# Layer 0's opening cut by batch: batch 0's keys and queries first, the rest among the attention units

## The reference

```python
x = x + _L0_xattn_ref(_layernorm(x), ctx_4096, ctx_4096, Wq, bq, Wk, bk, Wv, bv, Wo, bo)

Q = query @ Wq + bq; K = key @ Wk + bk; V = value @ Wv + bv   # 32 heads of 16; 8 key heads
scores = einsum('bhgqd,bhkd->bhgqk', Q, K) * scale
w = softmax(scores, axis=-1)
y = einsum('bhgqk,bhkd->bqhgd', w, V).reshape(B, S, EMBED)
return y @ Wo + bo
```

## Time and profile before

| | us |
|---|---|
| median of 3 runs | 1238.02 |
| fastest, slowest run | 1235.65, 1238.74 |
| the profiled execution's own time | 1236.24 |
| its span, first to last instruction | 1234.6 |
| TensorE busy | 1184.4 (96%) |
| VectorE, ScalarE, GpSimd busy | 818.9, 671.0, 404.5 |

### The profile page before, as it was taken

The page is one execution under the profiler, slowest core; times in us unless marked ns, Lnnn a source line. Parts: engine busy times, 40 slices in busy tenths (PEclk is TensorE's granted clock), DMA queues, the critical chain, the costliest instruction groups (busy, mean ns, idle before and its releaser), DMA issues.

```text
span 1234.6 us, 16581 instructions
## 1 busy us (share of the span) xinstructions
PE 1184.4 (96%) x5948; PEld 914.7 (74%) x5948; DVE 818.9 (66%) x1543; ACT 671.0 (54%) x1562; POOL 404.5 (33%) x483
## 2 busy tenths in 40 slices
PE   8989889899999999899999999999999999999997
...
PEclk9899999999999999899999999999999999999999
...
GB/s 290 173 172 134 139 91 103 284 217 102 153 203 253 150 147 181 86 59 60 60 44 69 43 61 69 61 52 54 69 59 50 44 69 60 61 69 27 59 1 68
DMA packets 72849, 127.93 MB, mean 104 GB/s; under 512 B 11640, under 2 KB 30968, under 8 KB 70072
## 3 DMA queue, kind: packets, MB, share of 16 engines
...
...
## 4 chain that ended last, share of the span: by engine, by line
PE 80%; DVE 8%; DMA 5%; ACT 3%; issue 3%; SPq 1%; ACTq 0%; POOL 0%; POOLq 0%; DVEq 0%
PE bank L466 49%; PE bank L1198 11%; PE bank L1986 7%; PE bank L1962 4%; PE bank L678 2%; PE bank L1258 2%; PE bank L692 1%; DMA q0st<-m0T 1%; PE bank L2301 1%; PE bank L1219 1%; PE bank L644 1%; DMA wf_raw<-in_wffn,weight_row 1%; PE bank L659 1%; DMA x<-in_x 1%; DVE den L895 1%
## 5 line engine op out<-in xcount | busy, mean ns | idle before, releaser
L1954 POOL TENSOR_SCALAR p<-p,mx 128x256 f32<-128x256 f32 x256 | 163.2, 654 | 522.0 <-DVE mx L1948 522.0
L1165 DVE TENSOR_TENSOR wf_lo<-wf_raw,wf_hi 128x512 fp32r<-128x512 f32 x188 | 121.7, 690 | 33.4 <-ACT wf_hi L1159 28.6
L1940 ACT ACTIVATE p<-bank,mx 128x256 f32<-128x256 f32 x256 | 118.0, 485 | 10.7 <-DVE mx L1930 10.6
L466 PE MATMUL bank<-xnA_hi,w1q_hi 128*128 128x512 f32 x288 | 118.8, 413 | 3.7 <-DVE xnA_lo L460 3.2
L1159 ACT ACTIVATE wf_hi<-wf_raw 128x512 fp32r<-128x512 f32 x192 | 110.2, 626 | 9.0 <-DMA wf_raw<-in_wffn,weight_row 9.0
L466 PE MATMUL bank<-xnA_hi,w1q_lo 128*128 128x512 f32 x288 | 115.0, 399 | 0.0
L466 PE MATMUL bank<-xnA_lo,w1q_hi 128*128 128x512 f32 x288 | 114.4, 397 | 0.0
L1969 ACT ACTIVATE p1T_hi<-bank 128x512 fp32r<-128x512 f32 x128 | 75.1, 596 | 65.7 <-PE bank L1962 65.7
L1894 ACT ACTIVATE q1T_hi<-bank 128x512 fp32r<-128x512 f32 x64 | 38.2, 597 | 132.5 <-PE bank L466 132.5
L1900 DVE TENSOR_TENSOR q1T_lo<-bank,q1T_hi 128x512 fp32r<-128x512 f32 x64 | 44.2, 691 | 93.2 <-ACT q1T_hi L1894 93.2
L466 PE MATMUL bank<-w1o_hi,a1T_hi 128*128 128x512 f32 x256 | 105.2, 411 | 0.1
...
## 6 DMA issues: line engine op xcount, KB each, us to landing
w_raw<-in_wq SPq DMA_DIRECT2D x64, 256.0 KB
w_raw<-in_wo SPq DMA_DIRECT2D x64, 256.0 KB
moe<-xn SPq DMA_DIRECT2D x2, 2304.0 KB, 11.7
...
q0st<-q_rows SPq DMA_DIRECT2D x14, 256.0 KB, 4.7
x<-in_x SPq DMA_DIRECT2D x8, 256.0 KB, 5.2
...
q_rows<-q0T_hi ACTq DMA_DIRECT2D x8, 256.0 KB
```

The costliest lines, as they stand in the source:

```text
L466: ins = nc.tensor.matmul(ps, a, b, start=(n == 0), stop=(n == len(pairs) - 1))
L1165: nc.vector.tensor_tensor(wf[m % 2][1][:, a, c, :], raw[m % STREAMS][:, a, c, :], wf[m % 2][0][:, a, c, :].bitcast(F32), ALU.subtract).the ...
L1940: ins = nc.scalar.activation(pr1[s % 2][:, h, :], banks.of(("s1", s, n))[:, hh * 2 * P:(hh + 1) * 2 * P], ACT.Exp, bias=m[:, UH + h:UH + h ...
L1954: ins = nc.gpsimd.tensor_scalar(pr1[s % 2][:, h, :], pr1[s % 2][:, h, :], m[:, 3 * UH + h:3 * UH + h + 1], 1.0, ALU.mult, ALU.mult)
```

## The change

Layer 0's opening is cut into three pieces in place of two halves (`PIECES`): batch 0 alone, batches 1 to 3, batches 4 to 7. Tile 0 is normalised and turned alone, and its keys and four query blocks (128 columns wide) are multiplied, stored and loaded back before tiles 1 to 3 are normalised. Then follow batches 1 to 3 (blocks of 384 columns), of which the fourth query block stands behind unit 2. All four values of the first half and the turning of the second half's tiles stand behind the first batch's maxima, the second half's keys behind unit 9, its queries behind units 11, 15, 19 and 22, its values behind units 23 to 26. The statistics of the second half's tiles stand between the maxima of units 3 to 6 on VectorE, the rounding of the output weights between the first exponentials on ScalarE. SP's loads are ordered by this, and those of x and of the context for the second half are issued behind batch 0's keys and queries.

```diff
--- before.py
+++ after.py
-        QUERY_AT = {KV0 + 2: 1, KV0 + 4: 2, LEAD_S + 5: 3}
-        QUERY_OUT_AT = {3: 0, KV0 + 3: 1, KV0 + 5: 2, LEAD_S + 6: 3}
+        QUERY_AT = {KV0 + 3: 0, KV0 + 7: 1, KV0 + 11: 2, KV0 + 14: 3}
+        OUT_WEIGHT_AT = {KV0 + 4 + k: k for k in range(KT)}
+        KEYS_AT, STATS1_AT = KV0 + 1, 3
...
+        PIECES = [(0, 0, P), (0, P, HT), (1, 0, HT)]
+        KEY_STORED, QUERY_STORED = ("st_q3", "st_k", "st_k"), ("st_q2", None, "st_q_half1")
...
-            for b in range(HB):
-                load(x[:, b, :], A["x"][b]).then_inc(S[f"rows_in{b}"], 16)
-            load(wq[:, :, :], A["wq0"]).then_inc(S["ld_wq0"], 16)
+            load(x[:, 0, :], A["x"][0]).then_inc(S["rows_in0"], 16)
             load(wkv[:, 0], A["wkv0"][:, 0]).then_inc(S["ld_wk0"], 16)
-            load(ctxT[0][:, :, :], A["ctxT"][0]).then_inc(S["ld_ctx00"], 16)
+            load(ctxT[0][:, :, 0:P], A["ctxT"][0, :, :, 0:P]).then_inc(S["ld_wk0"], 16)
             load(bq[:, :], A["bq0"]).then_inc(S["ld_bqk0"], 16)
             load(bk[:, :], A["bk0"]).then_inc(S["ld_bqk0"], 16)
+            load(wq[:, :, :], A["wq0"]).then_inc(S["ld_wq0"], 16)
+            for b in range(1, HB):
+                load(x[:, b, :], A["x"][b]).then_inc(S[f"rows_in{b}"], 16)
+            load(ctxT[0][:, :, P:HT], A["ctxT"][0, :, :, P:HT]).then_inc(S["ld_ctx00"], 16)
             load(wkv[:, 1], A["wkv0"][:, 1]).then_inc(S["ld_wv0"], 16)
...
-            for b in range(HB, B):
-                load(x[:, b, :], A["x"][b]).then_inc(S["ld_x_rest"], 16)
-            load(ctxT[1][:, :, :], A["ctxT"][1]).then_inc(S["ld_ctx01"], 16)
-            load(bo[:, :], A["bo0"].broadcast_to([P, D])).then_inc(S["ld_wbo0"], 16)
-            load(wo_raw[:, :, :], A["wo0"]).then_inc(S["ld_wbo0"], 16)
...
+            keys_in(0)
+            queries_in(0)
+            for b in range(HB, B):
+                load(x[:, b, :], A["x"][b]).then_inc(S["ld_x_rest"], 16)
+            load(ctxT[1][:, :, :], A["ctxT"][1]).then_inc(S["ld_ctx01"], 16)
             keys_in(1)
             queries_in(1)
             maxima(0)
+            load(bo[:, :], A["bo0"].broadcast_to([P, D])).then_inc(S["ld_wbo0"], 16)
+            load(wo_raw[:, :, :], A["wo0"]).then_inc(S["ld_wbo0"], 16)
...
-        VALUES_AT = {KV0 - 1: (HB, HB + 1), KV0: (HB + 2,), KV0 + 1: (HB + 3,)}
+        VALUES_AT = {3 * KV0 - 1 + k: HB + k for k in range(HB)}
...
-            for k in range(HB):
+            norm_turn(0, 0, 0)
+            keys(0, 7)
+            for m, n in enumerate((4, 5, 6, 0)):
+                query(0, m, n)
+            for k in range(1, HB):
                 norm_turn(0, k, k)
-            query(0, 0, 4)
-            query(0, 1, 5)
-            keys(0, 7)
-            query(0, 2, 0)
-            query(0, 3, 1)
-            for b, n in enumerate((2, 3, 4, 5)):
-                values(b, n)
-            for k, n in enumerate((7, 2, 3, 4)):
-                norm_turn(1, k, n)
             keys(1, 5)
-            query(1, 0, 7)
+            for m, n in enumerate((7, 2, 3)):
+                query(1, m, n)
             for i in range(-LEAD_S, UNITS0 - KV0 + ADD_LAG + 1):
                 if i + LEAD_S < UNITS0:
                     scores(i + LEAD_S)
                 if 0 <= i + LEAD_T < UNITS0:
                     turned_scores(i + LEAD_T)
                 j = i + LEAD_S
-                for b in VALUES_AT.get(j, ()):
-                    values(b, b - HB + 2)
+                if j == 2:
+                    query(1, KT - 1, 4)
                 if j == KV0 - 1:
                     maxima(0)
+                    for b, n in enumerate((2, 3, 4, 5)):
+                        values(b, n)
+                    for k, n in enumerate((7, 2, 3, 4)):
+                        norm_turn(1, k, n)
+                if j == KEYS_AT:
+                    keys(2, 5)
                 if j in QUERY_AT:
-                    query(1, QUERY_AT[j], 7)
+                    query(2, QUERY_AT[j], 7)
+                if j in VALUES_AT:
+                    values(VALUES_AT[j], next(srs))
...
-            norm_sqrt(0)
-            for k in range(HB):
-                norm_hi(0, k)
-            query(0, 0)
-            act.wait_ge(S["q0_lo"], 1)
-            queries_out(nc.scalar, 0, 0)
-            query(0, 1)
-            act.wait_ge(S["q0_lo"], 2)
-            queries_out(nc.scalar, 0, 1)
+            norm_sqrt(0, 0, 1)
+            norm_hi(0, 0)
             keys(0)
             act.wait_ge(S["k0_lo"], 1)
             keys_out(nc.scalar, 0)
-            norm_sqrt(1)
-            query(0, 2)
-            act.wait_ge(S["q0_lo"], 3)
-            queries_out(nc.scalar, 0, 2)
-            for k in range(KT // 2):
-                out_weight(k)
-            query(0, 3)
-            act.wait_ge(S["q0_lo"], 4)
-            queries_out(nc.scalar, 0, 3)
-            for k in range(KT // 2, KT):
-                out_weight(k)
-            for k in range(HB):
-                norm_hi(1, k)
+            for m in range(KT):
+                query(0, m)
+                act.wait_ge(S["q0_lo"], m + 1)
+                queries_out(nc.scalar, 0, m)
+            norm_sqrt(0, 1, HB)
+            for k in range(1, HB):
+                norm_hi(0, k)
             keys(1)
-            query(1, 0)
+            act.wait_ge(S["k0_lo"], 2)
+            keys_out(nc.scalar, 1)
+            for m in range(KT - 1):
+                query(1, m)
+                act.wait_ge(S["q0_lo"], KT + m + 1)
+                queries_out(nc.scalar, 1, m)
             for i in range(-LEAD_S, UNITS0 - KV0 + ADD_LAG + 1):
                 if 0 <= i + LEAD_T < UNITS0:
                     softmax_exp(i + LEAD_T)
                 j = i + LEAD_S
+                if j == 2:
+                    query(1, KT - 1)
+                    act.wait_ge(S["q0_lo"], 2 * KT)
+                    queries_out(nc.scalar, 1, KT - 1)
                 if j == KV0 - 1:
+                    norm_sqrt(1)
                     maxima(0)
                     nc.scalar.activation(preload[:, :], eps, ACT.Exp)
+                    for k in range(HB):
+                        norm_hi(1, k)
+                if j == KEYS_AT:
+                    keys(2)
                 if j in QUERY_AT:
-                    query(1, QUERY_AT[j])
-                if j in QUERY_OUT_AT:
-                    act.wait_ge(S["q0_lo"], KT + QUERY_OUT_AT[j] + 1)
-                    queries_out(nc.scalar, 1, QUERY_OUT_AT[j])
+                    query(2, QUERY_AT[j])
+                if j - 1 in QUERY_AT:
+                    m = QUERY_AT[j - 1]
+                    act.wait_ge(S["q0_lo"], 2 * KT + m + 1)
+                    queries_out(nc.scalar, 2, m)
+                if j in OUT_WEIGHT_AT:
+                    out_weight(OUT_WEIGHT_AT[j])
...
-            for k in range(HB):
+            dve.wait_ge(S["rows_in0"], 16)
+            norm_stats(0, 0)
+            norm_recip(0, 0, 1)
+            norm_scale(0, 0)
+            keys(0)
+            for m in range(KT):
+                query(0, m)
+            for k in range(1, HB):
                 dve.wait_ge(S[f"rows_in{k}"], 16)
                 norm_stats(0, k)
-            norm_recip(0)
-            for k in range(HB):
+            norm_recip(0, 1, HB)
+            for k in range(1, HB):
                 norm_scale(0, k)
-            query(0, 0)
-            dve.wait_ge(S["ld_x_rest"], 16 * HB)
-            norm_stats(1, 0)
-            norm_stats(1, 1)
-            query(0, 1)
-            norm_stats(1, 2)
-            keys(0)
-            norm_stats(1, 3)
-            query(0, 2)
-            norm_recip(1)
-            norm_scale(1, 0)
-            query(0, 3)
-            for k in range(1, HB):
-                norm_scale(1, k)
-            for b in range(HB):
-                values(b)
             keys(1)
+            for m in range(KT - 1):
+                query(1, m)
             for i in range(-LEAD_S, UNITS0 - KV0 + ADD_LAG + 1):
                 if i + LEAD_S < UNITS0:
                     softmax_max(i + LEAD_S)
                 j = i + LEAD_S
                 if j == 2:
-                    query(1, 0)
-                for b in VALUES_AT.get(j, ()):
-                    values(b)
+                    query(1, KT - 1)
+                if 0 <= j - STATS1_AT < HB:
+                    if j == STATS1_AT:
+                        dve.wait_ge(S["ld_x_rest"], 16 * HB)
+                    norm_stats(1, j - STATS1_AT)
                 if j == KV0 - 1:
                     maxima(0)
+                    for b in range(HB):
+                        values(b)
+                    norm_recip(1)
+                    for k in range(HB):
+                        norm_scale(1, k)
+                if j == KEYS_AT:
+                    keys(2)
                 if j in QUERY_AT:
-                    query(1, QUERY_AT[j])
+                    query(2, QUERY_AT[j])
+                if j in VALUES_AT:
+                    values(VALUES_AT[j])
...
```

(6 more changed lines are left out.)

133 lines of the change are left out of this document (74 added, 59 removed).

## The result

The changed kernel takes 1254.27 us in the median (1253.78 to 1255.12, 4 runs); the kernel before, on the same chip in the same rounds, 1238.38 (1235.65 to 1240.29, 4 runs). The ratio is 1.0131, interval 1.0117 to 1.0146: 15.9 us slower, against a sum of 14.3 and a forecast of 1251 (1241 to 1257). The time lies in the range, but above the forecast's own band (1247 to 1253). The profiled execution has a span of 1252.5 us.

What follows compares the result with a forecast made beforehand. TensorE, busy 96% of the span, was taken as the bound. 7.5 to the second maxima + 7.2 + 1.4 - 1.8 = + 14.3 on 1236.24 gives 1250.5, 1252.3 by the median; put at 1251, range 1241 to 1257.

Steps and rivals of the forecast that it cites:

- (b): Rival: batch 0's detour through memory comes late by 2 to 6 us, 1253 to 1257; 0.14, shared with a longer train.
- Hole one: TensorE idle from 14.6 to 22.6 us, before tile 1 is turned: 8.0 us, between 4.6 and 12.1.
- the train: Batch 0's blocks: rounding on ScalarE, remainder on VectorE, two store issues, then the next rounding; 1.92 us each, five in a row.
- The clock: TensorE's granted clock falls to half after each of the two holes, costing 2.4 us each, 0 to 3.4.
- Hole two: TensorE waits for VectorE's maxima 3 to 7 and four statistics between them, 40.3 to 48.3 us: 6.8 us.
- The wait for the exponential: Before the second maxima, the fourth transposed scores wait for ScalarE's second exponential: about 2.2 us of idleness.
- Behind the second maxima: Extra TensorE work of 7.2 us, two short waits of 1.4, one old wait gone, minus 1.8.
- the wait ahead of unit 32: The kernel's 1.81 us wait for batch 4's keys goes, as values stand in between: minus 1.8.
- the sixth exponential: One of two short waits behind the second maxima: 0.7 us of the 1.4.
- (a): Rival: the clock holds through both holes or falls only for a moment; + 9.5 us, 1246; chance 0.18.
- (c): Rival: faster, holes hardly open (under 2 and 3 us); at most 9.8 us won, 1229; chance 0.07.
- (d): Rival: no change, holes at lower ends (4.6 and 6.4), clock holds; + 0.1, 1238; 0.11 with what lies near.

Runs made afterwards that it cites:

- a_issue: Changed kernel with batch 0's ten stores issued by SP's queue instead of ScalarE's; 1252.76 us, ratio 1.0126.
- a_fill: Changed kernel with dummy transposes on TensorE in both holes, whose results nothing waits for; 1250.42 us, ratio 1.0093.
- b_fill: Kernel before with four dummy transposes in each of units 1 to 6; 1237.94 us, ratio 0.9994.
- a_st1: Changed kernel with the second half's statistics moved on VectorE from between maxima 3 to 7 to between remainders of batches 1 to 3; 1251.59 us.
- a_vals: Changed kernel with the four values moved ahead of batch 0's turned maxima on TensorE; 1250.34 us, ratio 1.0094.
- a_stats: Changed kernel with statistics of tiles 1 to 3 among the remainders of batch 0's blocks, root and copies moved likewise; 1254.21 us, ratio 1.0136.

## Why the prediction was right, point by point

The measured 1254.3 lies above the band of the forecast (1247 to 1253, given 0.50), in that of "(b) or a longer train" (1253 to 1257, given 0.14). It was the longer train, not (b). The way to the number was right in its mechanism; that the stages agree so well is in part luck, as follows.

**Hole one** was forecast at 8.0 us and is 9.4. The term that was mis-sized is the train: 2.03 us for 1.92, since rounding and remainder take 0.37 and 0.35 at 128 columns (I had taken 0.31 and 0.29 from other operations), and two of the first issues took 1.16 instead of 0.59. That is 1.5 us; TensorE was done 0.35 sooner, and three tiles' statistics took 2.4 for 2.8. a_issue shows the mechanism: without the issues in the train 4.4 us remain. The blocks of 384 columns took 2.48 for 2.6 and the clock cost 2.1 for 2.4, which gave most of it back: first scores at 37.11 for 37.0. That agreement is errors that cancel.

**The clock** falls after both holes, as said. Its price was put at 2.4 for each; TensorE worked 4.3 us at half clock behind hole one and 3.4 behind hole two, half of it lost, 2.1 and 1.7, and a_fill gives 3.8 for both at the second maxima (3.9 by the medians). The price was read off the one fall before, and b_fill got back only 1.8 there. The Trainium skill (TensorE: Matmul & The Clock Gate, HAM oscillation) prices a fall at half of its throttled time. Here the clock was at half for 10.3 us at hole one, 5.1 by that rule; the trace does not agree, because TensorE had no work in the larger part of it.

**Hole two** ends as forecast, but by luck: VectorE was done with the last query block at 42.14 (forecast 41.5) and took 6.2 us for maxima and statistics (forecast 6.8; a tile's statistics took 0.8 and not 0.93), so it ends at 48.3, and the row of the first maxima is at 48.45. a_st1 and a_vals show both halves of the cause, the statistics between the maxima and the values behind them.

**From there to the second maxima** the forecast was 74.0 and the row is 74.76. The turns came 1.2 us sooner, mostly since less clock was lost. The wait for the exponential is 1.3 and not 2.2, but a third fall of the clock, which I had not seen coming, makes a query block of 3.60 us one of 5.01, and the short matmuls and waits around it take about 1 us more than I had counted.

**Behind the second maxima** +6.8 was forecast (7.2 + 1.4 - 1.8) and +7.0 is there, to the fifth maxima. No experiment isolates this part; it is read from the windows. The windows of this stretch, of after:

```profile
74.76:120.38 45.62, 42.58 (x263) 25.42 (x261) 29.80 (x52) 20.83 (x43) 14.86 (x18) 0.96 0.61 151
```

and of before:

```profile
66.53:105.16 38.63, 34.58 (x224) 19.21 (x222) 26.82 (x46) 19.27 (x41) 3.71 (x9) 1.00 0.71 180
```

The idleness went from 4.05 to 3.04 us, -1.0 where -0.4 was forecast: the wait ahead of unit 32 is gone as said, and the sixth exponential makes none. The clock, in no term, costs 45.62 x 0.04 = 1.8, nearly all behind the wait for the fourth maxima (1.95 us for 1.13). The rest, 6.2, is the work, for which 7.2 was given. Three terms are off by 0.6 to 1.8 and cancel: luck again.

**The rest**, that nothing later absorbs the loss, holds: +0.1 to the experts, and the 15.9 us of the medians are the 15.3 at the experts' turn, within what runs differ. The forecast stood 1.3 below what its own sum and median gave (1252.3), with no reason named.

**The rivals.** (a) is out: the clock did fall; a_fill is (a) made true, and its 1250.4 is above the 1246 given, because hole one was longer, the third and fourth falls stayed, and a part of the gain was lost again behind the second maxima. (b) did not happen in the changed kernel, whose first scores wait for no load. It was near, though: a_stats brings it about by moving the turns 5 us ahead. The Trainium skill (Perfetto Trace Analysis, DMA Optimizations) says that transfers under 2 KB carry a large overhead; the store of 512-byte lines took 2.17 us there, less than the 7.15 of the wide one. So no such cost showed, but the store is of 64 KB where the wide one is of 256 KB, and no run holds the size and changes the lines. (c) asked for holes under 2 and 3 us; they were 9.4 and about 6. (d) asked for a hole one at its lower end (4.6) and a clock that holds; neither came.
